# A graph layer with a graph-attention gate: flat scans by chunk, zero and weight transfers spread over chunks, the end of the sort in steps, units and table split moved at the seam

## The reference, cut to what matters

```python
# x (6250, 256), src/dst (200000,) sorted by dst, edge_index (2, 131072) unsorted
def gnn(x, W, M, src, dst):
    agg = segment_sum((x @ M)[src], dst, num_segments=6250)
    return relu(x @ W + agg)

def ffn(x, ...):                     # HEADS = 4, NUM_EXPERTS = 4, TOP_K = 2
    h = (x @ W_gat).reshape(M, HEADS, NUM_EXPERTS)
    # src, dst: edge_index and one loop per node
    a_src, a_dst = (h * att_src).sum(-1), (h * att_dst).sum(-1)
    e = leaky_relu(a_src[src] + a_dst[dst], 0.2)
    ee = exp(e - segment_max(e, dst)[dst])
    alpha = ee / (segment_sum(ee, dst)[dst] + 1e-16)
    agg = segment_sum(h[src] * alpha[:, :, None], dst) + b_gat
    scores = layernorm(agg).reshape(M, HEADS, NUM_EXPERTS).mean(1)
    w = softmax(top2(scores))
    return sum_e gate_e * (gelu(x @ W1[e] + b1[e]) @ W2[e] + b2[e])

x = x + gnn(layernorm(x), W, M, src, dst)
x = x + ffn(layernorm(x), ...)
```

## Time and profile before

| | us |
|---|---|
| median of 3 runs | 3039.76 |
| lowest run | 3037.41 |
| the profiled execution | 3039.66 |
| its span | 3038.4 |
| PE busy | 2402.1 (79%) |
| DVE busy | 2252.1 (74%) |
| POOL busy | 2200.3 (72%) |
| ACT busy | 541.7 (18%) |

### The profile page before, as it was taken

The page is one execution under the profiler, slowest core; times in us unless marked ns, Lnnn a source line. Parts: engine busy times, 40 slices in busy tenths (PEclk is TensorE's granted clock), DMA queues, the critical chain, the costliest instruction groups (busy, mean ns, idle before and its releaser), DMA issues. The chain is left out here.

```text
span 3038.4 us, 42695 instructions
## 1 busy us (share of the span) xinstructions
PE 2402.1 (79%) x13244; PEld 1878.2 (62%) x13244; DVE 2252.1 (74%) x6360; ACT 541.7 (18%) x938; POOL 2200.3 (72%) x2260
## 2 busy tenths in 40 slices
PE   1466887878877878879888888988789999999723
PEld 0344565655655556557666666656579988888713
DVE  6589878877887656577666666666367999999958
ACT  4000121112112333322111111111100110011112
POOL 3677777777777777777777777777777777777760
PEclk9777998989999999989999999999899999999957
DMA  8977777777777777768877777877612222222188
GB/s 270 331 231 217 227 226 225 221 228 226 231 226 235 237 240 233 225 214 256 251 240 247 240 250 241 251 243 236 183 30 49 68 66 52 68 65 62 45 265 261
DMA packets 477160, 600.92 MB, mean 198 GB/s; under 512 B 72654, under 2 KB 415750, under 8 KB 474886
## 3 DMA queue, kind: packets, MB, share of 16 engines
q1 hardware_dynamic: 378886, 376.33, 37.6%
q0 software_dynamic: 97600, 220.02, 26.2%
q10 hardware_dynamic: 448, 1.85, 0.2%
HBM read 312.82 MB, written 286.79 MB: 197 GB/s over the span
## 5 line engine op out<-in xcount | busy, mean ns | idle before, releaser
L1544 POOL DMA_INDIRECT ring<-xn_d,srci x1611 | 1576.8, 979 | 514.5 <-issue 452.5
L776 DVE SCALAR_TENSOR_TENSOR ring<-ring,same_v,wide 128x256 f32<-128x256 f32 x1610 | 770.0, 478 | 564.1 <-PE wide L1352 460.0
L1352 PE MATMUL wide<-ring,one_hot 128*128 128x256 f32 x3222 | 916.5, 420 | 281.9 <-DMA ring<-xn_d,srci 171.4
L1352 PEld LDWEIGHTS wide<-ring,one_hot 128*128 128x128 f32 x3222 | 641.0, 208 | 514.6 <-DMA ring<-xn_d,srci 210.9
L1579 POOL DMA_INDIRECT g<-tab_d,srt x512 | 507.0, 990 | 156.1 <-issue 153.4
L1454 PE MATMUL wide<-tab_parts,low_hot 128*128 128x208 bf16 x6144 | 565.1, 253 | 50.3 <-DVE low_hot L818 50.2
L1454 PEld LDWEIGHTS wide<-tab_parts,low_hot 128*128 128x128 bf16 x6144 | 545.8, 98 | 71.2 <-DVE low_hot L818 63.4
L1410 PE MATMUL wide<-w2s,hh 128*128 128x256 f32 x1568 | 386.8, 391 | 1.5 <-DVE yo L754 1.5
L1400 PE MATMUL wide<-xt,w1s 128*128 128x512 f32 (+1 forms) x832 | 387.2, 589 | 0.8 <-DVE feat L744 0.8
L713 DVE TENSOR_SCALAR one_hot<-iota_f,dloc 128x128 f32<-128x128 f32 x1611 | 361.9, 304 | 3.2
L1157 ACT ACTIVATE hh<-wide,b1c 128x512 f32<-128x512 f32 (+1 forms) x208 | 137.9, 663 | 1215.7 <-PE wide L1400 1215.3
(11 more groups left out here) (359 smaller groups left out, 1444.2 us busy)
## 6 DMA issues: line engine op xcount, KB each, us to landing
run_d<-ring SPq DMA_DIRECT2D x201, 1024.0 KB, 5.3
ring<-xn_d,srci POOLq DMA_INDIRECT x1611
y_d<-yo SPq DMA_DIRECT2D x196, 128.0 KB, 2.6
comb<-y_d SPq DMA_DIRECT2D x28, 896.0 KB, 11.6
low_row<-low_d SPq DMA_DIRECT2D x16, 1024.0 KB
sum_d<-g SPq DMA_DIRECT2D x16, 768.0 KB, 3.9
g<-tab_d,srt POOLq DMA_INDIRECT x512
xn_d<-ring SPq DMA_DIRECT2D x7, 896.0 KB, 5.2
```

The costliest lines, as they stand in the source:

```text
L776: dve_at["run", j] = step(V.scalar_tensor_tensor(out=o, in0=ring[:, (j - 1) // JC % RING, (j - 1) % JC, :], scalar=same_v[:, j:j + 1], in1 ...
L1352: T.matmul(wide[:, 4 + j // 2 % 2, j % 2 * D:(j % 2 + 1) * D], one_hot[:, j // 4 % 4, j % 4, :], ring[:, j // JC % RING, j % JC, :], start ...
L1544: G.indirect_dma_start(out=ring[:, s, j % JC, :], out_offset=None, in_=xn_d, in_offset=at_rows(srci[:, j:j + 1])).then_inc(sem(f"gather{s} ...
```

## The change

- `weigh` and `sum_up` work on new tiles with the row's elements side by side (`logit`, `fade`, `reset_c`, `by_row`), each row with a 65th element at its front that carries the last chunk's value. One scan then runs flat over four rows (260 elements); `reset_c` and `fade` cut the rows apart. Scans: 1 instead of 4 for the maxima, 5 instead of 20 for the sums.
- ScalarE copies the results to `g`, four rows at a time (`copy_rows`, six copies a chunk), and SP's store waits for the copies. The edge scans (line 870) stay. `SUMMED_STEPS` falls from 28 to 22. GpSimd no longer waits for the sums, only for the store.
- At chunk 3 SP only writes the zero row of `run_d`. The table's zeros go at chunks 4 and 5, those of `start_d` at 9 to 12 and the weight loads one per chunk at 9 to 16.
- The end of the sort is five steps instead of one, with the digits split off as `digits_of`.
- Eight units (348 to 355: four hidden ones of job 44 = (11, 0), i.e. tiles 44 to 47 with expert 0, and four of y) are moved to chunk 204, at the head of the loop body on every engine, before `turn_sums(48)`. `FIRST_UNITS` falls from 16 to 8.
- `split_table` and the first low columns are cut in seven pieces and taken after each of those eight first units.

```diff
-FIRST_UNITS = 16
+FIRST_UNITS = 8
-SUMMED_STEPS = 28
+SUMMED_STEPS = 22
+    ZERO_AT, WEIGHTS_AT = 4, 9
+    GAP_UNITS = 8
+    ENDS = 4
+    AFTER_MERGES = ENDS + 1 + 2 * NT + 3
+    gap_chunk = ready(NT - 1) + 3
+    units_at_visits, units_1 = units_1, units_1 + GAP_UNITS
...
             then(V.tensor_single_scalar(key_i[:, :], key_i[:, :], (1 << KEY_BITS) - 1, ALU.bitwise_and))
+            yield
...
             then(V.tensor_tensor(same_f[:, 1:C2], key_i[:, 1:C2], key_i[:, 0:C2 - 1], ALU.is_equal))
+            yield
...
-            V.wait_ge(sem("zero_out"), ZERO_OUT)
-            row_tables(sm[:, 3:4], key_i[:, :], other, C2)
+            yield
+            digits_of(key_i[:, :], other, C2)
+            yield
+            V.wait_ge(sem("starts_zero"), STARTS_ZERO)
+            V.wait_ge(sem("table_zero"), TABLE_ZERO)
+            V.wait_ge(sem("run_zero"), 16)
+            row_tables(sm[:, 3:4])
...
         for c in range(NCH + AFTER):
+            if c == gap_chunk:
+                for _ in range(units_1 - sum(late_after)):
+                    next(mlp)
...
-        for _ in range(units_1 - sum(late_after)):
-            next(mlp)
...
-            for h in range(HEADS):
-                if h % 2 == 0:
-                    yield
-                step(V.tensor_tensor_scan(g[:, s, :, FE + h], reset_c[:, c % 2, :], g[:, s, :, HX + h],
-                                          -BIG if c == 0 else before_top[:, :, h], ALU.add, ALU.max))
+            if c >= 1:
+                V.wait_ge(sem("rows_copied"), ROW_COPIES * c)
+            dve_at["topped", c] = then(V.tensor_tensor_scan(
+                flat(rows_top), flat(reset_c[:, :, :]), flat(logit[:, :, :]), 0.0, ALU.add, ALU.max))
...
-            for f in range(FE):
-                if f % 2 == 0:
-                    yield
-                h = f // NX if f < HX else f - HX
-                step(V.tensor_tensor_scan(g[:, s, :, f], st[:, :, h], g[:, s, :, f],
-                                          0.0 if c == 0 else g[:, (c - 1) % GR, FC - 1:FC, f], ALU.mult, ALU.add))
+            for e in range(NX + 1):
+                yield
+                rows = flat(by_row[:, e * HEADS:(e + 1) * HEADS, :])
+                dve_at["scanned", c, e] = step(V.tensor_tensor_scan(rows, flat(fade[:, :, :]), rows, 0.0,
+                                                                    ALU.mult, ALU.add))
             dve_at["summed", c] = step.settle()
+            if c + 1 < NCF:
+                then(V.tensor_copy(by_row[:, 0:FE, 0:1], by_row[:, 0:FE, FC:FC + 1]))
...
+        table = split_table()
+        for i, turn in enumerate(turns_2):
             if turn == "unit":
                 next(mlp)
+                if i < min(FIRST_UNITS, left):
+                    next(table, None)
                 continue
...
+        def copy_rows(c):
+
+            o = g[:, c % GR, :, :]
+            A.wait_ge(dve_step, dve_at["topped", c])
+            A.activation(o[:, :, FE:FG].rearrange("p k f -> p f k"), by_row[:, FE:FG, 1:FC + 1],
+                         ACT.Copy).then_inc(sem("rows_copied"), 1)
+            for e in (*range(NX), NX):
+                A.wait_ge(dve_step, dve_at["scanned", c, e])
+                o_e = o[:, :, HX:FE].rearrange("p k h -> p h k") if e == NX else (
+                    o[:, :, 0:HX].rearrange("p k (h e) -> p e h k", e=NX)[:, e, :, :])
+                A.activation(o_e, by_row[:, e * HEADS:(e + 1) * HEADS, 1:FC + 1],
+                             ACT.Copy).then_inc(sem("rows_copied"), 1)
...
         for c in range(NCH + AFTER):
+            if c == gap_chunk:
+                for _ in range(GAP_UNITS):
+                    next(mlp)
             for k in due(c, 3):
                 turn_sums(k)
...
             if c >= GR:
                 G.wait_ge(sem(f"sum_out{s}"), sent(c // GR - 1))
-                G.wait_ge(dve_step, dve_at["summed", c - GR + 1])
...
+            if ZERO_AT <= c < ZERO_AT + 2:
+                table = tab_d.rearrange("(p a) f -> p (a f)", p=P)
+                a, b = ((0, C2), (C2, NT * FG))[c - ZERO_AT]
+                Q.dma_start(table[:, a:b], zeros[:, 0:b - a]).then_inc(sem("table_zero"), 16)
+            if WEIGHTS_AT <= c < WEIGHTS_AT + FS:
+                k = c - WEIGHTS_AT
                 flat = start_d.rearrange("(p a) f -> p (a f)", p=P)
...
         def store_sums(c):
-            Q.wait_ge(dve_step, dve_at["summed", c])
+            Q.wait_ge(sem("rows_copied"), ROW_COPIES * (c + 1))
```

More of the change, by code:

```diff
@@ L544, in row_tables @@
             step(V.tensor_scalar(heads_at[:, 0, :], offs[:, :], -1.0, head, ALU.mult, ALU.add))
[L545 to L548, removed]
             step.settle()
@@ L856, in scores, with flat, first_columns @@
                                  AXX, ALU.add))
+        rows_e, rows_top = by_row[:, HX:FE, :], by_row[:, FE:FG, :]
+        def flat(rows):
+            return rows.rearrange("p f k -> p (f k)")
+        def first_columns():
+            step(V.memset(by_row[:, 0:FE, 0:1], 0.0))
+            step(V.memset(fade[:, :, 0:1], 0.0))
+            step(V.memset(reset_c[:, :, 0:1], -BIG))
+            step(V.memset(logit[:, :, 0:1], -BIG))
+            step.settle()
         def weigh(c):
             a, b, s, e = c * FC, (c + 1) * FC, c % GR, c % 4
-            e_, top_, st = g[:, s, :, HX:FE], g[:, s, :, FE:FG], step_f[:, c % 2, :, :]
-            before_top = None if c == 0 else g[:, (c - 1) % GR, FC - 1:FC, FE:FG]
+            now, last = slice(1, FC + 1), slice(0, FC)
             a_dest, same = edge[:, e, :, :], same_f[:, a:b]
@@ L873, in weigh @@
                     yield
-            if c >= 2:
-                V.wait_ge(dve_step, dve_at["summed", c - 2])
-            step(V.tensor_scalar(reset_c[:, c % 2, :], same, -1.0, BIG, ALU.add, ALU.mult))
+            step(V.tensor_scalar(reset_c[:, :, now], same_f[:, None, a:b].broadcast_to([P, HEADS, FC]), -1.0, BIG,
+                                 ALU.add, ALU.mult))
+            if c >= 1:
+                step(V.tensor_copy(logit[:, :, 0:1], rows_top[:, :, FC:FC + 1]))
             V.wait_ge(sem(f"feat_in{s}"), 16 * PC * (c // GR + 1))
@@ L894, in weigh @@
+            yield
+            if c >= 1:
+                V.wait_ge(sem("rows_copied"), ROW_COPIES * c)
+            dve_at["topped", c] = then(V.tensor_tensor_scan(
+                flat(rows_top), flat(reset_c[:, :, :]), flat(logit[:, :, :]), 0.0, ALU.add, ALU.max))
             yield
-            then(V.tensor_tensor(e_, e_, top_, ALU.subtract))
-            dve_at["weighed", c] = then(V.tensor_scalar(st, st, 0.0, None, ALU.min))
+            step(V.tensor_tensor(fade[:, :, now], rows_top[:, :, last], rows_top[:, :, now], ALU.subtract))
@@ L897, in weigh @@
+            then(V.tensor_tensor(logit[:, :, now], logit[:, :, now], rows_top[:, :, now], ALU.subtract))
+            dve_at["weighed", c] = then(V.tensor_scalar(fade[:, :, now], fade[:, :, now], 0.0, None, ALU.min))
             yield
@@ L1139, in sort_steps @@
                 yield
-            yield
+            for _ in range(ENDS + 1):
+                yield
             for t in range(NT):
@@ L1319, in sort_steps @@
                 yield
+            for _ in range(ENDS):
+                yield
             T.wait_ge(dve_step, dve_at["next"])
```

112 lines of the change are left out of this document (68 added, 44 removed).

## The result

| us | before | after |
|---|---|---|
| median of 20 runs each | 3038.78 | 3044.81 |
| lowest and highest run | 3033.12 to 4880.14 | 3040.45 to 3050.99 |
| the profiled execution | 3039.66 | 3043.14 |
| its span | 3038.4 | 3041.9 |
| DVE busy | 2252.1 | 2236.4 |

The ratio is 1.0021, 95% interval 1.0015 to 1.0028: 0.2% slower, some 6 us by the medians, 3.5 us by the two profiled spans.

A forecast was written before the change was run, and what follows sets the result against it. GpSimd's chain of gathers was taken as the bound. From 3039.7 us, -8.7 (zeros, weights), -6.0 (sort end), +18.8 (seam), -1.0 (tail) and -3 (gathers) gave 3039.8, so 3040 us, range 3014 to 3062.

The forecast's parts named there:

- Zeros and sort end: First layer, ahead of the seam: spreading zeros and weights gains 8.7 us, the sort end in steps 6.0 us.
- the slack of 5.5 us: Ring at the sort end: a VectorE burst of 11.5 us cost GpSimd only 6.0, so 5.5 us were covered.
- The seam: Between the stages: eight units ahead of the last tile's transposes delay the head row's gather, +18.8 us, ends 0 and 24.
- Table split: Start of the second stage: units cover TensorE's 12.38 us idle, but the table's read-back comes 18.8 us later; worth nothing.
- Tail: Behind the last gather: six flat scans save 1.4 us, one copy adds 0.4; net -1.0 us, ends -4 and +0.5.
- the prediction's other estimate: Flat scan's length by the built-in scan's half throughput: 0.70 us instead of 0.93, making the sum 1.4 us lower.
- Gathers beside the chunk work: Second layer: fewer, longer scans disturb GpSimd's gather calls less, -3 us, bounds -20 and +20.
- the 0.045 us of the earlier trace: Second-layer gather calls: 0.941 us before the first scans, 0.986 among them; chunk work costs GpSimd up to 20 us.
- The hole was not large enough: Rival at the seam: TensorE's hole holds the units, last tile not delayed, seam term 0, 3021 us; chance 0.14.
- The savings came: Rival ahead of the seam: savings don't come, burst moves to chunks 9 to 16, sort-end backlog stays, 3052 us; chance 0.16.
- Flat scans block nothing: Rival in the second layer: flat scans hold up gather calls, mean 1.11 us instead of 0.990, 3088 us; chance 0.05.
- The fourth, VectorE as the bound: Rival in the second stage: VectorE becomes the bound, needing 6.2 us more per chunk; no chance of its own given.

The follow-up runs named there:

- the run with 3.5 us more a chunk and 13.0 us of strides: Kernel after without moved units, columns innermost, plus five unread flat scans in each of 15 second-layer chunks: 3090.48 us, ratio 1.0159 to before.
- the run with the other xt: Kernel after, eight units in place, but the four of job 44 read group 10's inputs instead of group 11's: 3034.7 us, ratio 0.9974 to before.

## Why the prediction was right, point by point

3040 was forecast, with 3014 to 3062 around it; the medians say 3044.8. The mechanism was right in every large part, and the errors of the terms are small and partly of one sign.

- **Zeros and sort end, -14.7 us.** Measured -15.2 up to the last first-layer gather. That the slack of 5.5 us holds was right: 39 gathers in the window where some 40 were named, and no store wait over 1.4 us. Counted by gathers, the two parts gave 8.5 and 5.6 us, 14.2 together; the other 1.0 is the balance of small gains of 3.3 and a loss of 2.3 that the forecast did not have, and that is luck. No run on a chip with this bound has one of the two parts alone.
- **The seam, +18.8 us.** Measured +19.15, and 19.1 by taking the units out. By its steps: the load of xt was issued at 2157.70 us, where the earlier trace rows less 15.2 gives 2157.7; it landed after 3.9 us, estimated 4.6; the units took 16.3 us, estimated 16.0; the transposes came 20.9 us late, estimated 21.2; and from them to the head row it was 13.5 us, estimated 12.8. "The xt load carries 12 of the 18.8 us" was right too: 11.3, and the units' own time 7.8.
- **Table split, 0.** Right: measured from the last first-layer gather, the matrix work starts after 78.0 us, before after 78.6, and TensorE no longer idles ahead of it (12.38 us in the earlier trace rows).
- **Tail, -1.0 us.** Measured -0.4. The direction held by two errors that nearly cancel. The first is the flat scan, which takes 0.68 to 0.70 us, not 0.93: six of them, five in one run, take 3.76 us where the 24 short ones took 7.07, a gain of 3.3 and not 1.4. That fits the prediction's other estimate, 0.70 us, worked out from the half throughput that the Trainium skill's page DVE: opcode table, instruction layouts, handler registers and perf-mode slots states in its section Datapath and trigger behaviour. By its own terms, "2 cycles of 0.96 GHz an element", 260 elements would be only 0.54 us; the other 0.16 us of the estimate its text does not name. The second error goes the other way: the step that failed is the copy of "0.40 us each like its exponential of that size", and, beside it, the multiplications, for which the text had no term at all. The copies took 0.83 to 0.87 us and the multiplication 0.77 instead of 0.42, since the change turned their operands so that neighbouring elements lie 96 bytes apart in `g`. The multiplications cost 1.4 us more than before, the addition of line 919 0.4, and the stretch behind the last scan 1.0. With the heads innermost they took 0.61 to 0.67 us, and the tail was 1.8 us shorter than before.
- **Gathers beside the chunk work, -3 us.** Measured -0.2. The scan time fell by half a microsecond per four rows, and a call's mean stayed 0.990. Even 75 more flat scans moved it by 0.004. So the 0.045 us of the earlier trace rows come from something else, which no run here names, and that its price follows the scan time is the assumption that failed. The Trainium skill's page GPSIMD Engine Reference, section Specifications, has contention between VectorE instructions with two SBUF inputs and GpSimd; for these gathers the runs show none that flat scans would bring.
- **The sum.** The terms measured give -15.2 + 19.15 - 0.2 - 0.4 + 0.1 = +3.5 us, forecast +0.1. Nearly all of the difference is the 3 us credited to the gathers. The medians differ by 6.0; the profiled execution of before was 0.9 above its median and that of after 1.7 below, which is the spread of single executions.
- **The rivals.** The hole was not large enough (GpSimd idled 19.0 us). The savings came. Flat scans block nothing. The fourth, VectorE as the bound, was dismissed with a wrong price: "it would need 6.2 us more per chunk". The 35.2 us between its chunks are not its work with 6.2 us to spare; they are the pace at which it catches up with gathers that started ahead of it, nearly without pause. Its reserve is what it waits at the end, 3.6 us over 16 chunks before and 15.4 after, and the run with 3.5 us more a chunk and 13.0 us of strides went 65 us over. "In the middle chunks 41.4 - 35.2 = 6.2 us of spare time hide it all" failed likewise. It cost nothing, because the change lowered VectorE's work. By this reading 1 us more of it a chunk would have cost the kernel before some 12 us (16 less 3.6), an estimate that no run tests.

## What to carry to other kernels

A hole on one engine is only worth filling ahead of late work if the filler is there before the hole and ends before the late work's input comes; count the wait of the filler's own inputs, then its length, at the clock level that the hole leaves. The spare time of a stage that catches up is the wait at its end, not the difference of two pitches; spend it once. When rows are turned so that a scan runs flat, the operations around it pay for the strides, and the order of the innermost elements has to be chosen anew for each of them.

## What the runs showed of the hardware that was not expected

- A scan of 260 elements takes 0.68 to 0.70 us. In a row five of them took 3.06 us, 0.61 each, where twenty of 64 elements took 5.83, so one long scan for four short ones saves 0.55 us of 1.17. The short ones also ran over elements 96 bytes apart; how much of the saving is that, and how much the starts, no run shows.
- The same 256 elements of float32 cost a VectorE multiplication 0.42, 0.61 or 0.77 us, and a ScalarE copy 0.64 to 0.67 or 0.83 to 0.87 us, by how the innermost elements lie: the multiplication in the kernel before, both with four heads innermost, and both with columns innermost, 96 bytes apart in `g`.
- The eight units took 16.3 us behind 11.8 us of idle time, and 16.15 us without it. The granted clock in the run with the other xt was 1.00 while TensorE did little, and 0.58 when the units began (windows of all engines, columns as above):

```profile
2147.00:2151.00 4.00, 0.58 (x3) 0.20 (x2) 2.42 (x9) 0.88 (x3) 3.09 (x4) 1.00 0.66 214
2151.80:2155.80 4.00, 4.00 (x9) 2.00 (x9) 0.62 (x4) 0.23 (x1) 3.08 (x4) 0.58 0.50 148
2155.80:2159.80 4.00, 3.61 (x13) 2.12 (x12) 0.42 (x1) 1.91 (x3) 3.08 (x4) 1.00 0.49 135
```

- On some chips all kernels took 4340 us, with pauses at "issue" of TensorE, and there the bound is no longer GpSimd. A change tuned to the bound of one chip need show nothing on the other.
